# A gated cross-attention and expert block on one core: context in chunks, turns behind the weighted sum, left-over products moved, masked V later

## The reference

```python
qh, kh, vh = heads(layernorm(x) @ Wq.T), heads(ctx @ Wk.T), heads(ctx @ Wv.T)   # 16 heads of 16
attn = softmax(qh * 256 ** -0.5 @ kh.T, axis=over the 512 tokens)
attn = attn / attn.sum(over the 1601 context rows)
x = x + tanh(g_xattn) * (attn @ vh) @ Wo.T
# then layernorm, a router that takes the best 2 of 8 experts, gelu(x @ w1[e]) @ w2[e], and
x = x + tanh(g_ffn) * weighted sum of the two experts
```

## Time and profile before

| | us |
|---|---|
| median of 3 runs | 1835.78 (1834.70 to 1840.76) |
| the profiled execution | 1838.29, its span 1836.6 |
| PE busy | 1723.5 (94%) |
| DVE busy | 1404.3 (76%) |
| ACT busy | 1254.0 (68%) |
| POOL busy | 551.1 (30%) |

### The profile page before, as it was taken

How to read it: one execution, slowest core, us unless ns; L and a number is a source line. 1 busy time by engine, 2 the same in 40 slices (tenths; PEclk the granted TensorE clock), 3 DMA queues, 4 the chain that set the end, 5 groups by cost and what they waited for, 6 DMA issues and landing times.

```text
span 1836.6 us, 32552 instructions
## 1 busy us (share of the span) xinstructions
PE 1723.5 (94%) x10466; PEld 930.9 (51%) x10466; DVE 1404.3 (76%) x2320; ACT 1254.0 (68%) x3521; POOL 551.1 (30%) x830
## 2 busy tenths in 40 slices
PE   8899799899989989999998999989899999999997
PEld 5223233333333333333333333323899999999997
DVE  7889799799989979989998999997444444444442
ACT  5989799899989989999998999997111111111111
POOL 3241143343325234423422432212222222222222
PEclk9999899999999999999999999999899999999999
DMA  8638414712731571281175136328522222222222
GB/s 223 148 78 204 107 45 123 206 42 59 208 84 51 149 183 33 78 235 45 52 191 134 45 99 166 116 89 216 165 37 36 37 36 36 37 36 36 37 34 29
DMA packets 138553, 182.12 MB, mean 99 GB/s; under 512 B 22112, under 2 KB 113376, under 8 KB 138432
## 3 DMA queue, kind: packets, MB, share of 16 engines
q1 hardware_dynamic: 123456, 159.67, 32.7%
q0 software_dynamic: 14144, 20.47, 6.6%
q10 hardware_dynamic: 832, 0.53, 0.1%
HBM read 126.69 MB, written 53.91 MB: 98 GB/s over the span
## 4 chain that ended last, share of the span: by engine, by line
PE 44%; DVE 23%; ACT 15%; issue 8%; DMA 6%; POOL 2%; SPq 1%; POOLq 0%; DVEq 0%; ACTq 0%
DVE negmax L1228 16%; ACT w_all L1022 14%; PE scores L1632 13%; PE scores L1645 13%; PE acc L834 6%; PE scores L807 5%; DMA w_all<-in_ctx_t 3%; PE spare L671 2%; PE spare L657 1%; DVE resid L1115 1%; PE acc L839 1%; DVE o_acc L1218 1%; DVE rz L1212 1%; DMA out<-row_t,gate_token 1%; ACT w_all L971 1%
## 5 line engine op out<-in xcount | busy, mean ns | idle before, releaser
L1022 ACT ACTIVATE w_all<-scores,negmax 128x512 f32<-128x512 f32 x1600 | 1083.4, 740 | 81.7 <-DVE negmax L1228 75.4
L1228 DVE TENSOR_REDUCE negmax<-scores 128x2 f32<-128x1024 f32 x809 | 968.9, 1206 | 73.4 <-PE scores L807 68.0
L807 PE MATMUL scores<-q_stack,w_all 128*128 128x512 bf16 x1536 | 482.4, 386 | 31.7 <-ACT w_all L1022 29.0
L834 PE MATMUL acc<-w_all,vz 128*32 128x512 f32 x3328 | 447.0, 609 | 1.0 <-POOL vz L1450 0.7
L1022 ACT ACTIVATION_READ_ACCUMULATOR w_all<-scores,negmax 128x1 f32 x1600 | 414.3, 259 | 0.0
L1678 ACT ACTIVATE projections<-scores 128x512 f32<-128x512 f32 x142 | 84.8, 597 | 447.3 <-PE scores L1632 447.3
L807 PEld LDWEIGHTS scores<-q_stack,w_all 128*128 128x128 bf16 x1536 | 125.0, 99 | 499.6 <-ACT w_all L1022 387.4
L1450 POOL TENSOR_TENSOR vz<-w_all,rz 128x68 f32<-128x68 f32 x416 | 124.7, 300 | 801.7 <-DVE rz L1212 751.3
L1632 PEld LDWEIGHTS scores<-row_t,q_stack 128*128 128x128 f32 x2272 | 264.4, 192 | 6.8 <-issue 1.7
L1632 PE MATMUL scores<-row_t,q_stack 128*128 128x128 f32 x2272 | 265.6, 275 | 1.6 <-DVE row_t L1705 1.4
L1645 PE MATMUL scores<-room,projections 128*128 128x256 f32 x1136 | 256.8, 379 | 0.0
(11 more groups left out here) (231 smaller groups left out, 1162.1 us busy)
## 6 DMA issues: line engine op xcount, KB each, us to landing
w_all<-k_parts SPq DMA_DIRECT2D x248, 204.4 KB, 3.8
w_all<-in_w SPq DMA_DIRECT2D x16, 1024.0 KB, 11.3
q_stack<-q_parts SPq DMA_DIRECT2D x248, 64.0 KB, 3.7
k_parts<-parts SPq DMA_DIRECT2D x42, 306.8 KB, 3.4
w_all<-in_ctx_t SPq DMA_DIRECT2D x7, 1635.0 KB, 8.4
parts<-routed SPq DMA_DIRECT2D x71, 129.0 KB, 2.1
q_parts<-parts SPq DMA_DIRECT2D x14, 384.0 KB, 4.0
routed<-pad_row SPq DMA_DIRECT2D x8, 645.0 KB, 9.7
```

The costliest lines, as they stand in the source:

```text
L807: mm = pe.matmul(scores[:, bank + j % 2, :], k_stacks[g][:, j, lt * P:(lt + 1) * P], q_stack[:, g, j, :], start=True, stop=True)
L834: mm = pe.matmul(acc[32 * j:32 * j + 32, :], vz[:, s % RING, j, :], probs[:, s % RING, j if lt < LT else j // 2, :], start=(lt == 0), stop ...
L1022: act.activation(lone_probs[:, :] if alone else probs[:, s % RING, j, :], scores[:, 2 * (u % SLOTS) + j % 2, :], ACT.Exp, bias=negmax[:, u ...
L1228: dve.tensor_reduce(negmax[:, u % 4, 0:n], scores[:, 2 * (u % SLOTS):2 * (u % SLOTS) + n, :], AX.X, ALU.max, negate=True).then_inc(negmax_ ...
```

## The change

Four things. (1) The context is loaded in four column chunks (`KCOLS`, 408 or 409 columns each), each with its own semaphore (`ctx_in`, which takes over `early_ctx`), and each as soon as the last V piece that reads its columns is taken: pieces 1, 3, 4 and 5 for the chunks 0 to 3 (`last_v_of`). K piece i waits for chunk i alone. In batch 0 all four chunks are issued behind own_v 6. (2) `begins_behind` also holds for turns (`TURNS`), so a turn that directly follows another piece stands behind `weigh`, and the second scores behind the turn. (3) From batch 1 on the left-over products of the groups 1, 2 and 3 are added where `weigh` runs in step 18, 37 and 50 (`LONE_BESIDE`), each a step with a turn, instead of 28, 41 and 2 of the next batch. Group 0, and all of batch 0, stay. (4) DVE takes v 6 and own_v 6 behind the second negmax of the step instead of between the two.

```diff
+TURNS = ("o_turn", "attn_turn", "row_turn", "x_turn")
+def weighs_lone(b, g):
+    return g * GROUP_STEPS + LT if b == 0 or g == 0 else LONE_BESIDE[g] - LAG
+LONE_BESIDE = {1: 18, 2: 37, 3: 50}
     def begins_behind(self, s):
-        begun = any(halves == (0,) for _, halves in self.halves(s))
+        begun = any(halves == (0,) or f[0] in TURNS for f, halves in self.halves(s))
         return begun and self.fill(s - 1) is not None and (s - LAG) % GROUP_STEPS > 0
+def last_v_of(c):
+    return min((KCOLS[c + 1] - 1) // (2 * P), VF - 2)
         def load_ctx(it):
-            sp.wait_ge(fill_taken, it.made("v", VF - 2))
-            sp.dma_start(ctx_sb[:, :, :], ctx_rows[it.b + 2]).then_inc(ctx_loaded, 16)
+            for c in range(KCHUNK):
+                cols = slice(KCOLS[c], KCOLS[c + 1])
+                sp.wait_ge(fill_taken, it.made("v", last_v_of(c)))
+                sp.dma_start(ctx_sb[:, :, cols], ctx_rows[it.b + 2][:, :, cols]).then_inc(ctx_in[c], 16)
@@ SP, batch 0
                 sp.wait_ge(fill_taken, it.made("own_v", VF - 1))
-                sp.dma_start(ctx_sb[:, :, :], ctx_rows[1]).then_inc(ctx_loaded, 16)
+                for c in range(KCHUNK):
+                    cols = slice(KCOLS[c], KCOLS[c + 1])
+                    sp.dma_start(ctx_sb[:, :, cols], ctx_rows[1][:, :, cols]).then_inc(ctx_in[c], 16)
@@ TensorE, fill
-                if i == 0 and 0 in halves:
-                    pe.wait_ge(ctx_loaded, (b + 1) * 16)
+                if i < KCHUNK and 0 in halves:
+                    pe.wait_ge(ctx_in[i], (b + 2) * 16)
@@ TensorE, weigh
-                               probs[:, s % RING, j if lt < LT else j // 2, :], start=(lt == 0), stop=False)
-            if lt == LT:
+                               probs[:, s % RING, j if lt < LT else j // 2, :], start=(lt == 0),
+                               stop=(lt == LT and s != weighs_lone(b, g)))
+            if s == weighs_lone(b, g):
                 pe.wait_ge(lone_vz_ready, lone_units(b, g))
@@ TensorE, run
                 if late:
                     weigh(it.b, s - LAG)
-                    unit_scores(it.b, s, 1)
+                    if not it.fill(s):
+                        unit_scores(it.b, s, 1)
                 for f, halves in it.halves(s):
                     fill(it, *f, halves)
+                if late and it.fill(s):
+                    unit_scores(it.b, s, 1)
@@ DVE, run
-                    if f and (f[0] not in ("v", "own_v") or f in LAST_V) and p == (f[0] in ("q", "k")):
+                    if f and (f[0] not in ("v", "own_v") or f in LAST_V) and p == (f[0] in ("q", "k", "v", "own_v")):
                         take(it, *f)
```

More of the change, by code:

```diff
@@ L359, in attention_and_routing @@
     x_loaded = sem("x_loaded")
-    ctx_loaded = sem("ctx_loaded")
     x2_loaded = sem("x2_loaded")
@@ L373, in attention_and_routing @@
     fill_taken = sem("fill_taken")
-    early_ctx = [sem(f"early_ctx_{c}") for c in range(KCHUNK)]
+    ctx_in = [sem(f"ctx_in_{c}") for c in range(KCHUNK)]
     early_k_in = [sem(f"early_k_in_{half}") for half in range(2)]
@@ L523, in first @@
                 cols = slice(KCOLS[c], KCOLS[c + 1])
-                sp.dma_start(ctx_sb[:, :, cols], ctx_rows[0][:, :, cols]).then_inc(early_ctx[c], 16)
+                sp.dma_start(ctx_sb[:, :, cols], ctx_rows[0][:, :, cols]).then_inc(ctx_in[c], 16)
             for w_sb, w, w_in in ((wv_sb, wv_t, wv_in), (wo_sb, wo_t, wo_in), (router_sb, router_t, wo_in)):
@@ L691, in first @@
                 if name == "k" and i < KCHUNK:
-                    pe.wait_ge(early_ctx[i], 16)
+                    pe.wait_ge(ctx_in[i], 16)
                 if (name, i) == ("x_turn", 0):
@@ L839, in weigh @@
                     mm = pe.matmul(acc[32 * j:32 * j + DH + 1, :], lone_vz[:, g * GH + j, :], lone_probs[:, :],
-                                   start=False, stop=True)
+                                   start=False, stop=(lt == LT))
             mm.then_inc(pv_done, 1)
```

## The result

| | before | after |
|---|---|---|
| median, same chip, 4 runs each | 1836.84 us (1834.70 to 1840.76) | 1805.22 us (1803.35 to 1806.20) |
| ratio after / before | | 0.9824, 95% interval 0.9805 to 0.9844 |
| profiled execution, its span | 1838.29, 1836.6 | 1806.20, 1804.5 |

The changed kernel is 1.8% faster. The forecast of 1812 was 7 us too slow, inside the range. Batches as windows, with the columns of the earlier trace rows: batches 0, 1, 4 and 7 of after.

The account below looks back on a forecast made before the run. ACT and DVE together bound a batch, with TensorE waiting for late context loads. -33.6 + 5.4 + 1.8 + 2.1 = -24.3 us takes 1838.3 to 1814.0; the median lies 2.5 lower: 1812 us, range 1801 to 1827.

Parts of the forecast that it names:

- Part 1: Context in four chunks: 33.6 us gained, ends 28 and 37; 32.8 in batches 1 to 6, 0.8 in batch 0.
- The 6.1 us: Start of batch 4: three steps last 15.3 us, would take 9.2 without the late load, so 6.1 gained.
- (c): Batch starts: chunks land later than the whole load did, the stall stays; 1845 us, chance 0.04.
- (d): Batch starts: SP reaches the load as late in every batch as in batch 1; 1825 us, chance 0.04.
- Part 2: Turns behind the weighted sum: costs and gains nothing, taken as 0, ends -3 and +3 us.
- Rival (b): Late turns cost in all steps, six more turns in six batches at 0.3 to 0.4 us; 1824 us, chance 0.17.
- Part 3: Lone products moved to steps 18, 37 and 50: 5.4 us lost at step 37, 1.8 at step 50.
- the shorter step 2: DVE's 0.66 us wait for the accumulator goes, against 1.0 lost in step 50; net 0.3 lost, six times.
- Part 4: Masked V behind the second row maximum in step 24: 0.3 us later, seven times, 2.1 us lost, ends -1 and 3.
- Batch 0: Its context wait of 1.3 us was to shrink, gaining 0.8 us.
- Rival (a): Lone products fit into gaps because ACT's backlog covers steps 37 and 50; 1802 us, chance 0.2.
- the signs named ahead: Context waits 28.1 to about 3 us; batches 2 to 6 152 to 153; ACT idles 0.9 and 1 in steps 37, 50.

Follow-up runs that it names:

- part 1 alone: The kernel before with only the context load split into four chunks; 1800.42 us, ratio 0.9878 to before.
- part 3 undone: The changed kernel with the lone products of groups 1 to 3 back at the ends of their groups; 1797.93 us, ratio 0.9867 to before.
- The last experiment: The changed kernel with chunk 0 issued among the stack loads, lone products behind the turn, and batch 0's x statistics earlier; 1786.08 us, ratio 0.9776 to before.
- parts 3 or 4 undone: Two kernels, each the changed one: lone products back at group ends (1797.93 us), or masked V back between the two row maxima (1799.63 us, ratio 0.9871).

## Why the prediction was right or wrong

**Part 1: right in size and mechanism.** Predicted 150.9 us for a batch with the chunks and the old rest; part 1 alone gives 150.97, its three steps 2.33 + 2.79 + 4.14 = 9.26 us against 9.2. The size holds for the first chip, where the waits of before had been read. On another chip TensorE waited 22.6 us for the context in before instead of 28.1, and the whole change is worth 26.4 us there. The 6.1 us that the late load had cost in batch 4, taken over from the trace "low clock included", were 4.38 us of wait and, by the comparison with batch 5, the clock for the rest. The clock does not fall after every such wait, as batch 5 shows. Batch 1 was to keep 5.5 and keeps 6.1 (157.22 - 151.11). Of these 5.3 are in its steps 0 and 1, where the load is late; most of the rest is step 2 with the lone products of batch 0. SP came to the chunk at 185.17, since batch 0 had lost 1.5 us. The landing took 5.2 us, as taken (5). Rivals (c) and (d) were wrong: no chunk of the batches 2 to 6 was waited for. The Trainium skill's rule that spoke against small loads ("DMA: Bandwidth & Descriptors", Bandwidth) cost nothing here: at the start of batch 1 the first 0.4 MB landed in 5.2 us and the last of the four chunks 10.1 us after the first was issued (195.28 and 185.17), where the whole had taken 11.1.

**Part 2: right, within its bounds.** Taken as 0, it costs 0.17 a batch, 1 us in all, from a gain of 0.15 and a cost of 0.32 in the steps with lone products. Rival (b) was wrong: DVE doesn't wait before its takes in steps 4, 5 and 19. In step 50 the turn behind `weigh` alone does cost 0.43 us (3.43 for 3.00, part 3 undone), but step 51 gives it back (1.67 for 2.10).

**Part 3: the term that was mis-sized.** 7.2 us predicted, some 0.6 measured. DVE's side came as computed: the second row maximum of step 37 begins 2.85 us behind the first, and the prediction had 625.4 - 622.54 = 2.86, the 622.54 being the first one in batch 3 of before. Two steps failed. The time at which ACT wants it was taken from before, 625.77, 3.23 us behind that first maximum; in the changed kernel ACT is further behind and would have wanted it 3.55 us behind, so it idles 0.56 and 0.51 us, not 0.9 and 1.0. And the shorter step 2 was credited with 0.66, without saying how it reaches ACT: ACT's waits for row maxima in steps 3 and 5 (0.21 and 0.44 with the products at the ends) become 0 and 0.16, so 0.49 comes back. 1.07 - 0.49 = 0.58; ACT's busy time is 0.24 less as well (144.32 and 144.08), and 0.34 remains where the batch shows 0.26. That step 41 gives nothing to the batch's end stands: it is 0.6 us shorter, and ACT had no gap to close there. What the prediction did not look at is the end of the kernel: the lone products of the last group had stood behind the last row maximum, and 1.46 us went with them. Nor did it put a price on batch 7, which is 0.5 us longer: in step 18 DVE waits 0.66 us for the turn and the step is 0.76 longer, steps 37 and 50 are 0.6 longer each, and steps 2, 28, 38 and 41 together give 1.8 back.

**Part 4: the sign was wrong.** +2.1 predicted in seven batches, -0.22 x 6 = -1.3 measured in six (batch 0 can't be read for it). Step 24 grew by 0.24, near the 0.3 of the working. What failed is "in a stretch that DVE bounds": ACT waits there too, for the second maxima of steps 24 and 26, and its first one came 0.16 sooner; and a DVE operation that GpSimd holds up became 0.28 us shorter by the shift. ACT's waits in steps 24 to 26 sum to 1.61 us where they were 1.69, and its busy time is 0.17 less; why it is less was not followed.

**Batch 0: missed.** It was to gain 0.8 and lost 1.5. It was ahead by 1.7 us at step 22, mostly from steps 7 and 10, and lost 3.2 in steps 23 and 24. The rows of after:

```profile
103.63 0.52 ACT L983 ACTIVATE parts<-spare 128x409 bf16<-128x409 f32 x1 [4.26 <-DMA k_parts<-parts]
...
104.89 1.97 PE L682 MATMUL spare<-projections,w_all 128*64 128x256 f32 x8 [4.88 <-DVE resid L1134]
```

ACT waits for the store of K piece 3, which lands 10.8 us after its issue, behind the 1024 writes of the statistics; in before it took 8.45 us and ACT waited 1.9. Of the 2.4 us more, 1.7 are that the store is issued sooner (92.72 and 94.40) and 0.7 that it lands later (103.54 and 102.85). TensorE then waits too, and its clock is low behind that (0.50 over 4 us; in before 0.57). The last experiment shows the cause of the wait. That the chunks alone make it longer is not shown: part 1 alone has 13.2 us in the two steps, parts 3 or 4 undone 11.1 and 11.2, on one chip, and in the changed kernel they are 14.4 on one chip and 12.0 on another. How much of the 1.5 us is the change's stays open.

**The sum.** Part 1 in six batches: 32.8 predicted. Batches 1 to 6 together gained 32.15 with all four parts, and parts 2 to 4 cost 0.13 in each, so part 1 alone comes to 32.15 + 6 x 0.13 = 32.9. Parts 2 to 4 were to cost 9.3 and come to 0.8 in six batches, 0.5 in batch 7 and -1.5 at the end, -0.2 in all: 9.5 us. Batch 0 took 2.3 back. 24.3 + 0.1 + 9.5 - 2.3 = 31.6 of the 32.1 us; another 0.4 lies in the expert stage, which the change doesn't touch. So the forecast was too slow because parts 3 and 4 were priced too high, and would have been more so had batch 0 not lost. Rival (a), 1802 us (its own terms give 1801), came nearer than the forecast, but not by its mechanism: the lone products do not fit into the gaps. Of the signs named ahead, the waits for the context, chunk 0's row, the wait of 0.66 us and the one that became 1.54 us came as said; batches 2 to 6 (151.1 for 152 to 153) and ACT's two waits did not.

## What to carry to other kernels

Split a load by what frees its target, and look at the issuing engine's program around it: what was left of the stall was SP's order, not bandwidth. When small work is moved beside a hand-over between engines, put it behind the hand-over: twice 1.04 us of it in front cost 1.03 us a batch. To price a delay, compute when the next engine wants the result in the changed schedule, and follow what the step that gets shorter frees on that engine.

## What the runs showed of the hardware

- A small DVE operation beside a GpSimd one ends when GpSimd's ends: 0.18 us alone, 1.32 and 1.04 here. It has two operands in SBUF, and so has GpSimd's. This is the rule of the Trainium skill ("SBUF — State Buffer", SBUF: two separate sides), an exclusive lock for a whole instruction; the trace agrees.
- 1024 writes of 4 bytes in two stores, 4 KB in all, delay a store of 307 KB, issued 5 to 6 us behind them, from 3.5 to between 8 and 10.8 us, from SP's queue. With the small ones on GpSimd's queue it is 13.2 us for a store issued 2 us behind them. A store issued 0.4 us ahead of them took 8.1. The Trainium skill ("DMA: Bandwidth & Descriptors", Issuing engines are not separate DMA queues) says that transfers interleave on the same engines whoever issues them; by the 13.2 us the trace agrees.
- TensorE's granted clock after a wait in batch 0, as windows of before and of after on one chip:

```profile
98.00:102.00 4.00, 1.55 (x14) 0.43 (x8) 2.00 (x4) 2.17 (x6) 0.65 (x2) 1.00 0.76 164
102.00:106.00 4.00, 4.00 (x30) 1.51 (x30) 2.82 (x5) 3.24 (x11) 0.73 (x2) 1.00 0.15 49
```
```profile
98.00:102.00 4.00, 0.89 (x6) 0.12 (x2) 1.08 (x3) 1.25 (x5) 0.30 (x1) 1.00 0.88 168
102.00:106.00 4.00, 3.74 (x14) 1.88 (x14) 1.33 (x2) 3.52 (x12) 0.87 (x1) 0.67 0.12 39
```

  After 2.45 us without work it stays at 2.4 GHz (1.00); after 3.37 us it is 0.67 over the 4 us from 102, so part of them at 1.2 GHz. The step that follows takes 4.30 us in the one and 5.94 in the other. Part 4 alone makes this step 0.25 longer (4.31 and 4.56 us in batch 4), so 1.4 us go with the clock. The length of the wait does not tell which it will be. Over the 4 us behind it the clock was 0.57 after 2.54 us in the same step of before on the first chip, 0.60 after 2.32 us with part 3 undone, and 1.00 after 3.08 us at the start of batch 5 of before.
